# Vision tower on one core: the last group's depthwise taps read PSUM through a ring of eight banks, and token codes go row by row

## The chip, the cores and the metric

One core of a Trainium2 chip runs the kernel. The metric is device time in microseconds. The engines are called by their short names in rows: PE is TensorE (matmul), PEld its weight load, DVE is VectorE, ACT is ScalarE, POOL is GpSimd, SP is SyncE, whose work here is to issue transfers.

## The reference

Sixteen images of 3 x 256 x 256 are turned into 257 tokens of 256 features each: Sobel gradients in x and y, their hypotenuse, summed over the channels, and one class token ahead. Then comes one transformer layer: layer norm and attention for the 27 tokens of largest energy, then layer norm and a feed-forward net whose two products have quantized activations and ternary weights:

```python
h = bit_linear(x, w1)                                # 256 -> 1024 channels, codes in 8 bits
h = depthwise_conv1d(h.transpose(0, 2, 1), conv_w, conv_b)   # 3 taps along the tokens, one filter a channel
h = h.transpose(0, 2, 1)
h = jax.nn.silu(h)
return bit_linear(h, w2)                             # scale: 127 / max |h| over a token's 1024 channels
```

The second product can't begin before the maximum over all 1024 channels of a token is known, and the result is added to the residual.

## The kernel before

The images are worked on in 4 groups of 4 (`GB = 4`). The instruction streams of the engines are written out by hand, with semaphores between them. In the first three groups the attention and the feed-forward net of group g are interleaved with the gradients of group g + 1; the last group has nothing beside it. Its feed-forward net is a stage of its own, and its order is what the change touches.

Token codes: VectorE writes nine rows of int16 codes (`token_codes`, L1097 and L1098), one increment of `zi_ready` at the last. ScalarE scales the nine rows (`tokens_scaled`, L1522), one increment of `zs_ready`. TensorE transposes them, 16 transposes in four banks and two more for the class token's row (L1908 and L1911), and ScalarE evicts each bank into `zT` (L1528, L1533). This piece is the same in all four groups.

Hidden layer: there are 8 tiles of 128 channels for each image, 32 in the group. TensorE makes a tile of 128 channels by 257 tokens with 4 matmul instructions (L1727) in one of four banks (A0, A1, B0, B1). In groups 0 to 2 ScalarE evicts it and TensorE does the three taps as products with diagonal matrices. In the last group (`convolve=False`) the taps are done by the other engines. VectorE copies a tile into `gpad`, a padded buffer of four tiles (L946), and increments `gd_ready`. ScalarE reads the copy and makes the middle tap with scale and bias (L1410, `mid_ready`). VectorE adds the left and right taps out of `gpad` with `scalar_tensor_tensor` (the helper `stt`, L565). Tiles go in pairs: `TILE_SLOTS` lists two tiles for each of eight slots, and taps of a pair come one slot behind its copies. A loop of two rounds handles two images in each.

When the eight tiles of an image are done (`y_conv`), ScalarE applies SiLU to all of them in two instructions (L1374, and L1375 for the class token) and increments `f_ready`; `TAIL_SILU` sets the slots in which it does. VectorE reduces the image to maxima over its channels (`hidden_maxima`, L951). In a round the first image's maxima are taken at the round's end, and those of the second images wait until both rounds are over, in `ffn_quantize`:

```python
with dve.Fori(0, 2) as j:
    w = Chain(dve, vtiles, j * TILE_STEPS, lag=1)
    for k in range(len(TILE_SLOTS)):
        ffn_tiles(w, gl, j, k)
    hidden_maxima(gl, 2 * j)
    dve.wait_ge(y_conv, 2 * j + 2)
    settle()
ffn_quantize(step, gl, range(1, GB, 2), lambda: None, lambda: None)
```

`Chain` makes an engine wait for its own earlier instruction, with lag=1 for the one before the last. After the maxima TensorE transposes them (L1739), VectorE makes scales (L966 to L973), TensorE spreads these (L1746), VectorE makes codes, ScalarE converts them (L1254), TensorE does the second product (L1758), VectorE adds it to the residual and SyncE stores (L471).

Of the kernel before, what the change touches and what calls it, by code (L numbers as in the profile page):

```python
# [44 lines left out]
TILE_SLOTS = tuple((2 * k, 2 * k + 1) for k in range(8)) + ((),)  # L45
TAIL_SILU = (5, 8)
GB = 4
# [77 lines left out]
def tower_kernel(nc, x, cls_tok, w_in, b_qk, b_v, w_out, b_out, w1, conv_w, conv_b, w2, const, out):  # L125
# [4 lines left out]
    TILE_STEPS = 30  # L130
# [6 lines left out]
    with ExitStack() as ctx:  # L137
# [80 lines left out]
        s2B = fmax  # L218
        again()
# [116 lines left out]
        vnorm = sem("vnorm"); vtiles = sem("vtiles")  # L336
# [44 lines left out]
        y_conv = sem("y_conv"); f_ready = sem("f_ready")  # L381
# [162 lines left out]
        def _(dve):  # L544
# [375 lines left out]
            def ffn_tiles(w, gf, j, k):  # L920


                conv, scale = TILE_SLOTS[k - 1] if k > 0 else (), TILE_SLOTS[k]
                nt = (gf * GB + 2 * j) * FT
                for tap in (0, 2):
                    for i in conv:
                        t = i % FT
                        yd, gp = (ydw, ydw_odd)[i // FT][:, t, :], gpad[:, i % 4, tap:tap + S]
                        if tap == 0:
                            dve.wait_ge(mid_ready, 2 * j * FT + i + 1)  # L930
                            w(stt(yd, gp, cw[:, t, tap:tap + 1], yd, ALU.mult, ALU.add))
                            if len(conv) == 1:
                                w.all()
                        else:
                            if t == FT - 1:
                                w.all()
                            ins = stt(yd, gp, cw[:, t, tap:tap + 1], yd, ALU.mult, ALU.add)
                            if t == FT - 1:
                                ins.then_inc(y_conv, 1)
                            else:  # L940
                                w(ins)
                for i in scale:
                    if conv and i % 4 == conv[-1] % 4:
                        w.all()
                    dve.wait_ge(g_psum, nt + i + 1)
                    v.tensor_copy(gpad[:, i % 4, 1:S + 1], (A0, A1, B0, B1)[i % 4][:, 0:S]).then_inc(gd_ready, 1)  # L946

            def hidden_maxima(gf, b):

                dve.wait_ge(f_ready, gf * GB + b + 1)  # L950
                return v.tensor_reduce(fmax[:, :, bass.ds(b, 1), :].rearrange("p j o r -> p j (o r)"),  # L951
                                       f4[:, :, :, bass.ds(b, 1), :].rearrange("p t j o r -> p j (o r) t"), AX, ALU.max,
                                       apply_absolute_value=True)

            def ffn_quantize(step, gf, batches, meanwhile_1, meanwhile_2):

                am, sc, dq = small2[:, 0, :], small2[:, 1, :], small2[:, 2, :]
                for b in batches:
                    ins = hidden_maxima(gf, b)
# [118 lines left out]
            def token_codes(step, g):  # L1078
# [112 lines left out]
            for g in range(1, GROUPS):  # L1191
# [9 lines left out]
                ffn_quantize(step, gl, range(GB), lambda: norm_mean(norm_step, ROWS, g),  # L1201
# [37 lines left out]
        def _(act):  # L1239
# [164 lines left out]
            def ffn_tiles(gf, j, k):  # L1404

                nt = (gf * GB + 2 * j) * FT
                for i in TILE_SLOTS[k]:
# [4 lines left out]
                if k in TAIL_SILU:  # L1412
                    half = TAIL_SILU.index(k)
                    act.wait_ge(y_conv, 2 * j + half + 1)
                    silu(gf, 2 * j + half, half, (ydw, ydw_odd)[half])
# [216 lines left out]
            with act.Fori(0, 2) as j:  # L1632
                for k in range(len(TILE_SLOTS)):
                    ffn_tiles(gl, j, k)
# [5 lines left out]
        def _(pe):  # L1640
# [63 lines left out]
            def feed_forward(g, convolve):  # L1704
# [16 lines left out]
                for b in range(GB):  # L1721
                    for t in range(FT):
                        i = b * FT + t
                        if i >= 4:
                            pe.wait_ge(gd_ready, g * (GB * FT) + i - 3)
                        for k in range(DT):
                            ins = mm((A0, A1, B0, B1)[i % 4][:, 0:S], w1q[:, k, t * P:(t + 1) * P], zT[:, k, b, :],  # L1727
# [15 lines left out]
                pe.wait_ge(gd_ready, (g + 1) * (GB * FT))  # L1743
# [56 lines left out]
            def attention(g):  # L1800
# [103 lines left out]
                pe.wait_ge(zs_ready, g + 1)  # L1904
                for i in range(4):
                    t, k = i // 2, i % 2
                    for j in range(4):
                        ins = tr((T0, T1, B0, B1)[i][:, j * P:(j + 1) * P], zs[:, 4 * k + j, t * P:(t + 1) * P], ident)  # L1908
                    ins.then_inc(zT_psum, 1)
                for t in range(DT):  # L1910
# [55 lines left out]
```

## Time and profile before

| | |
|---|---|
| time, median of 3 runs | 1516.29 us (1515.9 to 1517.93) |
| the profiled execution's own time | 1519.31 us |
| its span | 1517.5 us |
| instructions | 11197 |
| busy, share of the span | VectorE 87%, TensorE 54%, ScalarE 48%, GpSimd 11% |
| chain that ended last | VectorE 45%, ScalarE 12%, transfers 10%, TensorE 10%, issue 7% |

A busy share is a mean over stages that differ: VectorE is at nine tenths or more in most slices of the first 1290 us, and far below that in the last group's attention and feed-forward net. The granted clock of TensorE is given as a share of 2.4 GHz: 1.00 is that, 0.50 is 1.2 GHz.

### The profile page before, as it was taken

To read this page: it belongs to the slowest core of one execution; us is meant where nothing else is said; L and a number is where in the kernel's file an instruction comes from. 1 tells how busy PE (TensorE), PEld (TensorE's weight loads), DVE (VectorE), ACT (ScalarE), POOL (GpSimd) and SP (SyncE) were. 2 spreads that over 40 slices of the span, in tenths; PEclk is the share of its full clock that TensorE was granted. 3 is DMA by queue.
4 is the path that set the end of the run, shared out by engine and by line. 5 is a ranking of instruction groups with operands and counts; after the bars stand their busy time and mean duration, and the time that the engine had idled before them with its cause. 6 is when DMAs were issued, how large, how long until landed. Compare 5 with 4: busy or idle time off the path is not lost.

```text
span 1517.5 us, 11197 instructions
## 1 busy us (share of the span) xinstructions
PE 815.9 (54%) x3334; PEld 645.1 (43%) x3334; DVE 1320.9 (87%) x2024; ACT 728.9 (48%) x1300; POOL 166.2 (11%) x208
## 2 busy tenths in 40 slices
PE   3564200457548743457647842556547842696644
PEld 1332100345437632446536732445436642585523
DVE  7999998898999999998999989998999999423576
ACT  2222333156386744156476744256476743332662
POOL 0000000013213000012313000012303000000000
PEclk8886655667669866567579866567679866877876
DMA  8000600017437510126528510126528010100001
GB/s 205 1 14 15 118 1 0 1 25 114 81 59 128 116 42 0 29 39 101 92 46 134 111 42 1 29 40 99 98 41 132 7 42 0 28 1 1 0 0 28
DMA packets 46380, 78.13 MB, mean 51 GB/s; under 512 B 7490, under 2 KB 31730, under 8 KB 44658
## 3 DMA queue, kind: packets, MB, share of 16 engines
q0 software_dynamic: 33408, 50.34, 20.4%
q1 hardware_dynamic: 12338, 26.31, 7.5%
q10 hardware_dynamic: 576, 0.79, 0.2%
q8 instruction: 26, 0.43, 0.1%
q14 instruction: 32, 0.26, 0.1%
HBM read 22.84 MB, written 4.25 MB: 18 GB/s over the span
## 4 chain that ended last, share of the span: by engine, by line
DVE 45%; ACT 12%; DMA 10%; PE 10%; issue 7%; POOL 0%; SPq 0%; DVEq 0%; ACTq 0%
DVE arena L562 16%; DVE arena L565 14%; DMA arena<-nrows_mem 3%; DMA arena<-img 3%; ACT arena L1374 2%; PE psum L1715 2%; PE psum L1809 2%; DMA arena<-h 2%; DMA arena<-zT 2%; ACT arena L1247 2%; DVE red L578 1%; ACT arena L1512 1%; DVE arena L951 1%; DVE arena L1049 1%; DVE out L565 1%
## 5 line engine op out<-in xcount | busy, mean ns | idle before, releaser
L562 DVE TENSOR_TENSOR arena<-arena 128x768 f32<-128x768 f32 (+2 forms) x519 | 477.4, 975 | 26.3 <-ACT arena L1289 22.5
L565 DVE SCALAR_TENSOR_TENSOR arena<-arena 128x768 f32<-128x768 f32 (+2 forms) x224 | 202.2, 956 | 0.1
L1727 PE MATMUL psum<-zT,w1q 128*128 128x257 f32 x512 | 142.2, 414 | 19.4 <-DVE gpad L946 14.8
L1727 PEld LDWEIGHTS psum<-zT,w1q 128*128 128x128 f32 x512 | 105.4, 208 | 42.9 <-DVE gpad L946 19.9
L1831 PE MATMUL psum<-arena 128*128 128x257 f32 x128 | 55.9, 612 | 71.6 <-ACT arena L1490 53.3
L538 POOL DMA_DIRECT2D h<-others x60 | 52.4, 873 | 375.2 <-DVE others L565 286.1
L1715 PE MATMUL psum<-gpad,win 128*128 128x257 f32 x288 | 77.1, 406 | 26.1 <-ACT gpad L1388 26.1
L1326 ACT ACTIVATE arena<-arena 128x768 f32<-128x768 int16 x32 | 27.0, 843 | 124.2 <-DVE arena L565 123.5
L565 DVE SCALAR_TENSOR_TENSOR arena<-img 128x768 f32<-128x768 f32 x74 | 67.7, 954 | 9.0 <-DMA img<-x 8.7
L1715 PE MATMUL psum<-gpad,onehotT 128*128 128x257 f32 x216 | 58.0, 413 | 31.0 <-ACT gpad L1388 31.0
L1247 ACT ACTIVATE arena<-arena 128x256 f32<-128x256 f32 x65 | 23.3, 409 | 106.6 <-DVE arena L565 68.3
L1715 PEld LDWEIGHTS psum<-gpad,win 128*128 128x128 f32 x288 | 57.3, 202 | 38.7 <-ACT gpad L1388 29.8
L1831 PEld LDWEIGHTS psum<-arena 128*128 128x128 f32 x128 | 37.8, 310 | 84.4 <-ACT arena L1490 57.4
L951 DVE TENSOR_REDUCE arena<-arena 128x288 f32<-128x2304 f32 (+1 forms) x16 | 64.9, 4098 | 8.7 <-ACT arena L1375 8.5
L499 POOL DMA_DIRECT2D arena<-nrows_mem x18 | 15.6, 865 | 514.6 <-ACT arena L1298 442.2
L1391 ACT ACTIVATE xT<-psum,cb 128x257 f32<-128x257 f32 x96 | 45.5, 474 | 40.7 <-PE psum L1715 40.7
L1480 ACT ACTIVATE arena<-psum,arena 128x257 f32<-128x257 f32 x64 | 29.5, 473 | 68.0 <-DVE arena L1050 68.0
L1715 PEld LDWEIGHTS psum<-gpad,onehotT 128*128 128x128 f32 x216 | 44.3, 208 | 40.8 <-ACT gpad L1388 33.7
L565 DVE SCALAR_TENSOR_TENSOR arena<-arena,others 128x768 f32<-128x768 int16 x64 | 58.3, 953 | 0.0
L1662 PE MATMUL psum<-img,cst 128*128 128x512 f32 (+1 forms) x28 | 16.0, 713 | 73.2 <-DVE arena L565 73.2
L1374 ACT ACTIVATE arena<-xT 128x2048 f32<-128x2048 f32 (+1 forms) x14 | 55.2, 3941 | 0.2
L1775 PE MATMUL psum<-cst,arena 128*128 128x128 f32 x64 | 15.3, 402 | 73.7 <-DVE e L562 71.7
(235 smaller groups left out, 2121.6 us busy)
## 6 DMA issues: line engine op xcount, KB each, us to landing
arena<-nrows_mem POOLq DMA_DIRECT2D x36, 384.0 KB, 7.2
arena<-img POOLq DMA_DIRECT2D x36, 384.0 KB, 7.6
img<-x SPq DMA_DIRECT2D x36, 258.0 KB, 7.5
h<-others POOLq DMA_DIRECT2D x60, 128.0 KB, 2.7
arena<-arena POOLq DMA_DIRECT2D x18, 384.0 KB, 8.8
arena<-zT POOLq DMA_DIRECT2D x12, 384.0 KB, 8.4
out<-out SPq DMA_DIRECT2D x16, 256.0 KB
img<-x SPq DMA_DIRECT2D x48, 64.5 KB, 7.0
```

The source lines that it names most:

```text
L538: pool.dma_start(h9[:, row, :], others[:, row % 2, c, :], accum_op=ALU.add).then_inc(row_sums, 16)
L562: return v.tensor_tensor(o, a, b, op)
L565: return v.scalar_tensor_tensor(out=o, in0=a, scalar=s, in1=b, op0=op0, op1=op1)
L951: return v.tensor_reduce(fmax[:, :, bass.ds(b, 1), :].rearrange("p j o r -> p j (o r)"), f4[:, :, :, bass.ds(b, 1), :].rearrange("p t j o ...
L1247: ins = s.activation(ln[1][:, j, :], src(j), ACT.Square)
L1374: s.activation(fb[:, :, 0:ROWS, :], yd[:, :, 1:S].rearrange("p t (r j) -> p t j r", j=ROWS), ACT.Silu)
L1391: s.activation(ydw[:, t, :], (C0, C1, T0, T1)[i % 4][:, 0:S], ACT.Identity, bias=cb[:, t:t + 1]).then_inc(conv_taken, 1)
L1480: s.activation(attn[:, hg, :], (C0, C1, T0, T1)[hg][:, 0:S], ACT.Exp, scale=0.25, bias=sm[:, 1, hg:hg + 1], accum_out=sm[:, 2, hg:hg + 1]) ...
L1715: ins = mm((C0, C1, T0, T1)[i % 4][:, 0:S], diagonal(t, k), gpad[:, i % 4, k:k + S], start=(k == 0), stop=(k == 2))
L1727: ins = mm((A0, A1, B0, B1)[i % 4][:, 0:S], w1q[:, k, t * P:(t + 1) * P], zT[:, k, b, :], start=(k == 0), stop=(k == DT - 1))
L1809: ins = mm(C0[:, t * P:(t + 1) * P], y_row(j)[:, t * P:(t + 1) * P], rhs, start=(j == 0), stop=(j == ROWS))
L1831: mm((C0, C1, T0, T1)[hg][:, 0:S], qbd[:, hg // 2, 4 * (hg % 2):4 * (hg % 2) + 4, :].rearrange("p h q -> p (h q)"), kT[:, b % 2, hg // 2, ...
```

## The change

There are four edits. (1) In the last group TensorE puts its tiles in all eight banks in turn (`RING = 8`) and waits for `tile_done` of the tile eight before. The copy into `gpad` is gone: ScalarE's middle tap and VectorE's outer taps read the bank; the outer taps cover 256 columns. (2) The loop of two rounds is written out. SiLU of an image comes after the middle tap of tile 5 of the next image (`SILU_LAG = 5`), and its maxima after tile 7 of the next image. (3) The last image's SiLU and its maxima are made in two halves of four tiles each, and the two maxima are joined by one more instruction. (4) In all groups each row of token codes and each scaled row has its own increment and wait, and the transposes take rows 0 to 3 of both halves of the features first, then rows 4 to 7.

```diff
-TILE_SLOTS = tuple((2 * k, 2 * k + 1) for k in range(8)) + ((),)
-TAIL_SILU = (5, 8)
+RING = 8
+SILU_LAG = 5
...
+            def last_tiles(w, gf):
+                for i in range(0, GB * FT, 2):
+                    for j in (i, i + 1):
+                        t, g, y = j % FT, banks[j % RING], (ydw, ydw_odd)[j // FT % 2][:, j % FT, :]
+                        dve.wait_ge(mid_ready, j + 1)
+                        w(stt(y[:, 1:S], g[:, 0:S - 1], cw[:, t, 0:1], y[:, 1:S], ALU.mult, ALU.add))
+                    for j in (i, i + 1):
+                        t, g, y = j % FT, banks[j % RING], (ydw, ydw_odd)[j // FT % 2][:, j % FT, :]
+                        if j == i + 1:
+                            w.all()
+                        stt(y[:, 0:S - 1], g[:, 1:S], cw[:, t, 2:3], y[:, 0:S - 1], ALU.mult, ALU.add).then_inc(tile_done, 1)
+                    if i > FT and i % FT == FT - 2:
+                        w(hidden_maxima(gf, i // FT - 1))
...
+            def last_maxima(gf):
+                b, half = GB - 1, FT // 2
+                whole = fmax[:, :, b:b + 1, :]
+                dve.wait_ge(f_ready, gf * GB + GB)
+                image_maxima(fmax_low, b, slice(0, half)).then_inc(half_max, 1)
+                dve.wait_ge(f_ready, gf * GB + GB + 1)
+                image_maxima(whole, b, slice(half, FT)).then_inc(half_max, 1)
+                dve.wait_ge(half_max, 2)
+                return tt(whole, whole, fmax_low, ALU.max)
...
                 for row in range(ROW9):
-                    ins = v.tensor_scalar(zi[:, row, :], out9[:, row, :], nmean[:, row:row + 1], sc[:, row:row + 1],
-                                          ALU.add, ALU.mult)
-                ins.then_inc(zi_ready, 1)
+                    v.tensor_scalar(zi[:, row, :], out9[:, row, :], nmean[:, row:row + 1], sc[:, row:row + 1],
+                                    ALU.add, ALU.mult).then_inc(zi_ready, 1)
...
-            with dve.Fori(0, 2) as j:
-                w = Chain(dve, vtiles, j * TILE_STEPS, lag=1)
-                for k in range(len(TILE_SLOTS)):
-                    ffn_tiles(w, gl, j, k)
-                hidden_maxima(gl, 2 * j)
-                dve.wait_ge(y_conv, 2 * j + 2)
-                settle()
-            ffn_quantize(step, gl, range(1, GB, 2), lambda: None, lambda: None)
+            w = Chain(dve, vtiles, lag=1)
+            last_tiles(w, gl)
+            w.all()
+            ffn_quantize(step, gl, [lambda: last_maxima(gl)], lambda: None, lambda: None)
...
+            def last_tiles(gf):
+                nt = gf * (GB * FT)
+                for i in range(GB * FT):
                     t = i % FT
-                    act.wait_ge(gd_ready, nt + i + 1)
-                    s.activation((ydw, ydw_odd)[i // FT][:, t, :], gpad[:, i % 4, 1:S + 1], ACT.Identity,
+                    act.wait_ge(g_psum, nt + i + 1)
+                    s.activation((ydw, ydw_odd)[i // FT % 2][:, t, :], banks[i % RING][:, 0:S], ACT.Identity,
                                  scale=cw[:, t, 1:2], bias=cb[:, t:t + 1]).then_inc(mid_ready, 1)
+                    if i >= FT and i % FT == SILU_LAG:
+                        b = i // FT - 1
+                        act.wait_ge(tile_done, (b + 1) * FT)
+                        silu(gf, b, b % 2, (ydw, ydw_odd)[b % 2])
+                for half in range(2):
+                    act.wait_ge(tile_done, GB * FT - FT // 2 * (1 - half))
+                    silu_half(gf, GB - 1, half)
...
-                act.wait_ge(zi_ready, g + 1)
                 for row in range(ROW9):
-                    ins = s.activation(zs[:, row, :], zi[:, row, :], ACT.Copy, scale=token[:, 7, row:row + 1])
-                ins.then_inc(zs_ready, 1)
+                    act.wait_ge(zi_ready, g * ROW9 + row + 1)
+                    s.activation(zs[:, row, :], zi[:, row, :], ACT.Copy, scale=token[:, 7, row:row + 1]).then_inc(zs_ready, 1)
...
-                        if i >= 4:
+                        if convolve and i >= 4:
                             pe.wait_ge(gd_ready, g * (GB * FT) + i - 3)
+                        if not convolve and i >= RING:
+                            pe.wait_ge(tile_done, i - RING + 1)
+                        bank = (A0, A1, B0, B1)[i % 4] if convolve else banks[i % RING]
...
-                pe.wait_ge(zs_ready, g + 1)
                 for i in range(4):
-                    t, k = i // 2, i % 2
+                    k, t = i // 2, i % 2
+                    pe.wait_ge(zs_ready, g * ROW9 + 4 * k + 4)
```

## Rows read from the trace of the kernel before

**Rows 1.** Timeline, codes to the first hidden tile: start us, us, engine, line

```profile
1401.18 3.00 DVE L1098 TENSOR_SCALAR onehot<-out,token 128x256 int16<-128x256 f32 x9
...
1404.21 3.70 ACT L1522 ACTIVATE arena<-onehot,token 128x256 f32<-128x256 int16 x9 [4.51 <-DVE onehot L1098]
...
1407.97 3.68 PE L1908 MATMUL psum<-cst,arena 128*128 128x128 f32 x16 [15.46 <-ACT arena L1522]
1409.12 3.87 ACT L1528 ACTIVATE zT<-psum 128x512 f32<-128x512 f32 x4 [1.21 <-PE psum L1908]
...
1412.79 0.22 ACT L1533 ACTIVATE zT<-psum 128x4 f32<-128x4 f32 x2
...
1413.15 7.17 PE L1727 MATMUL psum<-zT,w1q 128*128 128x257 f32 x32 [1.09 <-ACT zT L1533]
```

**Rows 2.** Timeline, end of the hidden layer of the last group

```profile
1473.21 8.13 DVE L951 TENSOR_REDUCE arena<-arena  x2
...
1481.26 4.01 DVE L951 TENSOR_REDUCE arena<-arena 128x288 f32<-128x2304 f32 x1
1485.32 1.78 PEld L1739 LDWEIGHTS psum<-cst,arena 128*128 128x128 f32 x9 [22.42 <-DVE arena L951]
```

**Rows 3.** Windows: PE, PEld, DVE, ACT, POOL busy us (instructions), clock, DMA share

```profile
1413.00:1446.00 33.00, 21.25 (x81) 15.99 (x82) 24.59 (x52) 20.17 (x26) 0.00 (x0) 0.90 0.00 0
...
1120.00:1245.00 125.00, 83.23 (x347) 69.78 (x347) 118.77 (x142) 81.72 (x137) 19.50 (x24) 0.81 0.31 55
```

**Rows 4.** Timeline, one period of a pair of tiles

```profile
1420.23 0.75 DVE L946 COPY gpad<-psum 128x257 f32<-128x257 f32 x2
1420.69 1.09 ACT L1410 ACTIVATE xT<-gpad,cb,cw 128x257 f32<-128x257 f32 x2 [1.69 <-DVE gpad L946]
...
1421.33 1.77 DVE L565 SCALAR_TENSOR_TENSOR xT<-gpad,cw,xT 128x257 f32<-128x257 f32 x4 [0.34 <-ACT xT L1410]
1423.02 0.75 DVE L946 COPY gpad<-psum 128x257 f32<-128x257 f32 x2
```

**Rows 5.** VectorE's waits from 1413 to 1486: us in total, times, longest

```profile
DVE arena L565 <- ACT arena L1410: 10.5, 8, 4.3
DVE xT L565 <- ACT xT L1410: 4.2, 8, 1.9
```

**Rows 6.** Waits from 1120 to 1245, in the third group

```profile
ACT arena L1342 <- DVE arena L562: 5.6, 2, 3.5
...
DVE arena L951 <- ACT arena L1375: 2.4, 1, 2.4
```

**Rows 7.** Page, costliest groups: busy us, mean ns, idle before

```profile
L1391 ACT ACTIVATE xT<-psum,cb 128x257 f32<-128x257 f32 x96 | 45.5, 474 | 40.7 <-PE psum L1715 40.7
```

**Rows 8.** Line L565 by operands: ns min/median/max, first and last start

```profile
L565 DVE SCALAR_TENSOR_TENSOR arena<-arena,small x131: 475/480/485, 247.8 to 1282.8; 128x256 f32<-128x256 f32 x131
...
L565 DVE SCALAR_TENSOR_TENSOR out<-psum,small,out x36: 474/476/484, 610.1 to 1510.3; 128x256 f32<-128x256 f32 x36
```

**Rows 9.** Timeline, the result added to the residual out of PSUM

```profile
1507.13 3.62 DVE L565 SCALAR_TENSOR_TENSOR out<-psum,small,out 128x256 f32<-128x256 f32 x9 [1.68 <-PE psum L1758]
```

**Rows 10.** Timeline around the first SiLU of the last group

```profile
1430.31 1.28 ACT L1374 ACT_TABLE_LOAD   x1
...
1431.61 3.88 ACT L1374 ACTIVATE arena<-xT 128x2048 f32 x1
...
1435.93 1.08 ACT L1410 ACTIVATE arena<-gpad,cb,cw 128x257 f32<-128x257 f32 x2
...
1438.71 3.79 PE L1727 MATMUL psum<-zT,w1q 128*128 128x257 f32 x8 [4.71 <-DVE gpad L946]
```

**Rows 11.** Timeline, a strided reduction in the third group

```profile
1238.06 3.61 DVE L572 TENSOR_REDUCE red<-h 128x128 f32<-128x2048 f32 x1
```

**Rows 12.** Windows around the first hidden matmuls, columns as in rows 3

```profile
1408.00:1412.00 4.00, 4.00 (x18) 3.67 (x18) 0.00 (x0) 2.88 (x4) 0.00 (x0) 0.50 0.00 0
1412.70:1434.00 21.30, 17.17 (x72) 13.20 (x72) 15.52 (x38) 11.93 (x18) 0.00 (x0) 1.00 0.00 0
```

More of the change, by code:

```diff
@@ L129, in tower_kernel @@
     G_STEPS = 46
-    TILE_STEPS = 30
     IMG_IN = 16 * 2 * GB * CH
@@ L218, in tower_kernel @@
         s2B = fmax
+        fmax_low = take(ROW9 * SLOTS).rearrange("p (j o r) -> p j o r", j=ROW9, o=1)
         again()
@@ L334, in tower_kernel @@
         gpad_zero = sem("gpad_zero")
-        vnorm = sem("vnorm"); vtiles = sem("vtiles")
+        vnorm = sem("vnorm"); vtiles = sem("vtiles"); tile_done = sem("tile_done")
+        half_max = sem("half_max")
         h_saved = sem("h_saved")
@@ L380, in tower_kernel @@
         gd_ready = sem("gd_ready"); mid_ready = sem("mid_ready")
-        y_conv = sem("y_conv"); f_ready = sem("f_ready")
+        f_ready = sem("f_ready")
         fmax_ready = sem("fmax_ready"); fmaxT_psum = sem("fmaxT_psum"); fmaxT_taken = sem("fmaxT_taken")
@@ L918, in first_group @@
                 u.all()
[L920 to L946, printed above, removed]
@@ L948, in hidden_maxima, with image_maxima @@
+            def image_maxima(room, b, tiles):
+                return v.tensor_reduce(room.rearrange("p j o r -> p j (o r)"),
+                                       f4[:, tiles, :, b:b + 1, :].rearrange("p t j o r -> p j (o r) t"), AX, ALU.max,
+                                       apply_absolute_value=True)
             def hidden_maxima(gf, b):
                 dve.wait_ge(f_ready, gf * GB + b + 1)
-                return v.tensor_reduce(fmax[:, :, bass.ds(b, 1), :].rearrange("p j o r -> p j (o r)"),
-                                       f4[:, :, :, bass.ds(b, 1), :].rearrange("p t j o r -> p j (o r) t"), AX, ALU.max,
-                                       apply_absolute_value=True)
@@ L955, in ffn_quantize @@
-            def ffn_quantize(step, gf, batches, meanwhile_1, meanwhile_2):
+                return image_maxima(fmax[:, :, b:b + 1, :], b, slice(0, FT))
+            def last_maxima(gf):
[7 more added lines that the diff above has]
+                return tt(whole, whole, fmax_low, ALU.max)
@@ L957, in ffn_quantize @@
+            def ffn_quantize(step, gf, image_peaks, meanwhile_1, meanwhile_2):
                 am, sc, dq = small2[:, 0, :], small2[:, 1, :], small2[:, 2, :]
-                for b in batches:
-                    ins = hidden_maxima(gf, b)
+                for peak in image_peaks:
+                    ins = peak()
                 ins.then_inc(fmax_ready, 1)
@@ L1199, in _ @@
                 magnitude_rows(g, 3, lambda k: None)
-                ffn_quantize(step, gl, range(GB), lambda: norm_mean(norm_step, ROWS, g),
+                ffn_quantize(step, gl, [lambda b=b: hidden_maxima(gl, b) for b in range(GB)], lambda: norm_mean(norm_step, ROWS, g),
                              lambda: norm_variance(norm_step, ROWS, g * 2 + 1))
@@ L1402, in tap_diagonals, with silu_half @@
                 ins.then_inc(diagonals, 1)
-            def ffn_tiles(gf, j, k):
-                nt = (gf * GB + 2 * j) * FT
-                for i in TILE_SLOTS[k]:
+            def silu_half(gf, b, half):
+                tiles = slice(half * FT // 2, (half + 1) * FT // 2)
+                fb, yd = f4[:, tiles, :, b:b + 1, :].rearrange("p t j o r -> p t j (o r)"), ydw_odd[:, tiles]
+                s.activation(fb[:, :, 0:ROWS, :], yd[:, :, 1:S].rearrange("p t (r j) -> p t j r", j=ROWS), ACT.Silu)
+                s.activation(fb[:, :, ROWS, :], yd[:, :, 0:1].to_broadcast([P, FT // 2, BLK]), ACT.Silu).then_inc(f_ready, 1)
+            def last_tiles(gf):
+                nt = gf * (GB * FT)
+                for i in range(GB * FT):
                     t = i % FT
-                    act.wait_ge(gd_ready, nt + i + 1)
-                    s.activation((ydw, ydw_odd)[i // FT][:, t, :], gpad[:, i % 4, 1:S + 1], ACT.Identity,
+                    act.wait_ge(g_psum, nt + i + 1)
+                    s.activation((ydw, ydw_odd)[i // FT % 2][:, t, :], banks[i % RING][:, 0:S], ACT.Identity,
                                  scale=cw[:, t, 1:2], bias=cb[:, t:t + 1]).then_inc(mid_ready, 1)
[L1412 to L1415, printed above, removed]
+                    if i >= FT and i % FT == SILU_LAG:
[5 more added lines that the diff above has]
+                    silu_half(gf, GB - 1, half)
             def ffn_scales(gf):
@@ L1631, in _ @@
             tokens_scaled(gl)
-            with act.Fori(0, 2) as j:
-                for k in range(len(TILE_SLOTS)):
-                    ffn_tiles(gl, j, k)
+            last_tiles(gl)
             ffn_scales(gl)
@@ L1742, in feed_forward @@
                 pe.wait_ge(diag2_ready, g + 1)
-                pe.wait_ge(gd_ready, (g + 1) * (GB * FT))
+                if convolve:
+                    pe.wait_ge(gd_ready, (g + 1) * (GB * FT))
+                else:
+                    pe.wait_ge(tile_done, GB * FT)
                 for k in range(3):
@@ L1902, in attention @@
                     ins.then_inc(res_psum, 1)
-                pe.wait_ge(zs_ready, g + 1)
                 for i in range(4):
-                    t, k = i // 2, i % 2
+                    k, t = i // 2, i % 2
+                    pe.wait_ge(zs_ready, g * ROW9 + 4 * k + 4)
                     for j in range(4):
@@ L1909, in attention @@
                     ins.then_inc(zT_psum, 1)
+                pe.wait_ge(zs_ready, g * ROW9 + ROW9)
                 for t in range(DT):
```

2 lines of the change are left out of this document (1 added, 1 removed).

## The prediction

> **What bounds the kernel now.** I read the chain that ended last first: in the final 105 us the kernel has no next group to overlap with, so each stage there is on the path, while in the three groups before VectorE is nearly always busy. Then I took stage windows, the table of waits, and the timeline of the last group's hidden layer, which runs from the first matmul at 1413.15 to the last maximum at 1485.27: 72.1 us [rows 1, 2]. There no engine is full: in the first half VectorE works 24.6 of 33 us, TensorE 21.3, ScalarE 20.2 [rows 3]. What is seen instead is a handover. A pair of tiles takes 2.79 us (copy at 1420.23, next at 1423.02): 0.75 of copies, then 0.34 waiting for ScalarE's middle tap, then 1.68 of four outer taps [rows 4]. ScalarE reads the copy, so VectorE must copy first. Beside that each SiLU stops the taps, since ScalarE makes no middle taps meanwhile; the sum of VectorE's waits for it is 14.7 us, longest 4.3 [rows 5], and two reductions stand in a row at the end [rows 2]. In front of the stage lies a strictly serial piece: 9 code rows on VectorE, then 9 on ScalarE, then 18 transposes, then four evictions, 1401.18 to 1413.0 [rows 1].
>
> **Token codes row by row.** The first code row is done at 1401.6 instead of the ninth at 1404.2. ScalarE needs 3.70 for nine rows (0.40 apart), more than VectorE's 3.00, so it ends at 1401.63 + 3.70 = 1405.33, not 1407.91 [rows 1]. The order of transposes is changed to row halves: the first eight need rows 0 to 3, done at 1403.3; eight at 0.23 each end at 1405.2, the next eight at 1407.1, the two of row 8 at 1407.5. ScalarE evicts in order behind its ninth row: two quarters at once from 1405.3, 0.92 apart as now (four of 1.12 in 3.87), the third at 1407.2 at the latest, the fourth at 1408.1, then the two small ones: end about 1409.35. TensorE starts the hidden matmuls at 1409.45, **3.7 us** earlier than 1413.15. The added increments sit on instructions that are there anyway, and the added waits are met in order: behind ScalarE's wait for a row stand only the later rows and evictions. I cost them at nothing. In groups 0 to 2 the same 3.7 us are gained by ScalarE and TensorE but not by VectorE: ScalarE falls back into step at its next squares and roots, where it waits 5.6 us in all for VectorE's line L562 alone [rows 6]. So zero there. Bounds: VectorE's only wait at the group's end is 2.4 us (2.5 and 3.7 in the other two groups, of the same view), but the work that sets it starts after that 5.6 us wait, so I don't count it.
>
> **The ring and the dropped copies.** Removed: 32 copies (0.42 each, 0.32 to 0.43 on the engine [rows 4]), their handover, the loop with its settle memsets, and table loads at the loop's head. Added: nothing per tile; ScalarE's middle tap reads PSUM (0.47 for a like eviction with bias only [rows 7], 0.60 as now from SBUF; I take 0.50), VectorE's taps read PSUM and cover 256 columns. The trace has that form: 0.476 from PSUM against 0.480 from SBUF [rows 8], so the pitch of 0.42 (1.68 for four [rows 4]) stays; bounds are 0.39 (nine of the PSUM form in the last 3.62 us of VectorE's work: its pitch [rows 9]) and 0.48, no overlap at all. With clock full, TensorE needs 7.17/32 x 4, less its first fill, = 0.87 per tile [rows 1]. Now the recurrence, t = 0 at the first matmul. P is a tile's end in PSUM, M its middle tap, D its outer taps.
>
> Tiles 0 to 13: P13 = 1.1 + 13 x 0.87 = 12.4, M13 = 12.9. Taps of a pair cost 1.68 against TensorE's 1.74, so VectorE keeps up, one pair behind. Then SiLU of image 0: table load 1.28, and 4.32 from its start to the next middle tap (1431.61 to 1435.93 [rows 10]); M14 = 12.9 + 1.3 + 4.3 + 0.5 = 19.0. VectorE idles from 14.2 to 19.0: the one large stall that stays. TensorE fills the ring to tile 21 meanwhile.
>
> From 19.0 VectorE is the bound. Pair 7 ends at 20.7, maxima of image 0 take 4.06 [rows 2] to 24.8; ScalarE uses these to run to tile 21 (21.8), and does SiLU 1 until 26.1 with the table still loaded, hidden behind pairs 8 to 10, which end at 29.8. Pair 11 finds its middle taps (27.1) and ends at 31.5; maxima 1 to 35.6. The ring refills as pairs 8 to 11 free banks (26 to 31.5); even at half clock, 1.71 per tile (8 instructions in 3.79 [rows 10]), tile 29 is there by 36.8. At full clock M29 is at 34 and SiLU 2 ends at 38.3, before pair 15 starts at 40.6. Pairs 12 to 15 end at 42.3, maxima 2 at 46.4. The half SiLUs of image 3 (about 2.3 each, half of 4.32 and a fixed part) run from 39.2 and from 42.4, ended by 44.8: hidden. Last: two half reductions and one maximum of 288 elements. A strided reduction of 2048 elements to 128 costs 3.61 [rows 11], one of 2304 to 288 costs 4.02 [rows 2]: the price goes with elements, so 2.1 each; if it went with outputs, up to 2.8 each. 46.4 + 4.2 + 0.5 = **51.1**.
>
> **The clock.** When the transposes began at 1407.97 the granted clock was 0.50, and 1.00 from 1412.7 [rows 12], so the first hidden matmul ran at 2.4 GHz. Now they begin at about 1403.4 with a 2 us hole before the hidden matmuls. The clock may be up already, or rise up to 4.7 us into them. Each us at 1.2 GHz delays M13 by half a us: 0 to 2.3, I take **0.9**. A half clock later in the stage is covered by VectorE up to SiLU 2, see (d).
>
> The stage thus ends at 1409.45 + 51.1 + 0.9 = 1461.45 against 1485.27: **23.8 us** less, of which 3.7 from the token codes, about 20 from the ring. What follows (transposes of the maxima, scales, second product, store) is unchanged, after an idle TensorE in both. The sum against the profiled execution: 1519.3 - 23.8 = 1495.5 (span 1517.5, 1.8 around it). That execution was 3.0 above the median of the runs, so **1492.5** for the median.
>
> **A rule against the change.** Rows show PSUM no dearer than SBUF as a source of a VectorE tap, 0.476 against 0.480 [rows 8]. The Trainium skill ("VectorE: DVE Perf Modes", section "Rules for kernel authors") advises to copy PSUM to SBUF first where many operations follow, and its table in the section on the TRN2 errata gives a PSUM source 62 cycles more than an SBUF one, 65 ns as an estimate; over the 36 taps from pair 7 on that would be 2.3 us, a time of 1494.8. The rows disagree with the price, and by them the advice fails here: two taps and a middle tap don't repay a copy.
>
> **Rivals.** (a) Ring starved: the clock stays at 1.2 GHz. Then P29 = 2.1 + 29 x 1.71 = 51.7, SiLU 2 ends at 56.5, pair 15 at 58.7, and 4.1 + 4.2 + 0.5 more is 67.5, 16.4 over: 1508. Against it: 1.00 through 21 us with TensorE busy 17.2 of them [rows 12]. For it: 0.50 after each SiLU's hole [rows 10, 12]. (b) Table loads stay around each SiLU: +1.3 before M14, hidden at SiLU 1 (29.2 against 29.8), some 1.2 at SiLU 2: 1495. Against it: ScalarE goes from SiLU to the middle tap at 1435.93 without a load [rows 10]. (c) The other side: taps from PSUM get slow while ScalarE evicts and TensorE writes neighbouring banks. All 64 would have to cost 0.37 more, 0.80 in place of 0.42, to eat 24 us; beyond that it is slower, at 1.0 each it is 64 x 0.58 - 23.8 = 13 slower, 1529. Against it, copies from PSUM at 0.43 with TensorE writing [rows 4]; for it only that no tap has done this beside ScalarE. That the written-out loop starves for instructions has no sign in the earlier groups, which are written out too: VectorE is 118.8 of 125 us busy there [rows 3]. (d) The cover fails: SiLU 2 is late by TensorE at half clock (M29 37.4, M31 42.7): +1.5 to 2, in the range.
>
> **Numbers.** Forecast with (d) 0.80; (b) 0.07; (a) or part of it, 1498 to 1508, 0.08; (c) 0.03; gains beyond the sum (earlier groups' 2.4 to 3.7, faster pitch) 0.02. Low end: pitch 0.39 (-1.1), no clock loss (-0.9), middle taps and half reductions a bit cheaper (-0.5), rounded down to 1489. High end: clock +1.4, pitch 0.48 (+2.2), reductions by outputs (+1.4), together 1497.5, rounded to 1498. 0.2% is 3 us, about what a measurement here can tell from no change. Faster 0.96, same 0.02, slower 0.02.
>
> **What would show it.** Hidden matmuls start 3.7 us earlier after the codes. VectorE shows no copies, one wait of 4.5 to 5 us for the first SiLU, then is over 95% busy until the last maxima. Taps 0.48 long, 0.42 apart. One table load in the stage. The stage takes about 52 us; the last reductions are two of 2.1. It would be wrong if taps on PSUM are longer, if VectorE waits again at the second or third SiLU, or if the clock row reads 0.50 through the first 14 tiles.

## The result and the profile after

The changed kernel takes 1491.49 us (median of 4 runs, 1488.19 to 1494.95) against 1517.11 (1515.9 to 1518.31): a ratio of 0.9831, 95% interval 0.98 to 0.9862, 25.6 us less. (The before side is the three runs of the section on the time before and a fourth, 1518.31, which moves its median from 1516.29.) The changed kernel's runs lie in two pairs, 1488.2 and 1488.5, 1494.4 and 1494.95, so its median is a value between them that no run had. The profiled execution took 1488.19, of the lower pair; its span is 1486.4, 31.1 less than before.

The windows of the last group, columns as in [rows 3]: attention from the first energy maximum to the first code row, codes to the first hidden matmul, hidden layer to the transposes of the maxima, and the rest.

```profile
1291.82:1395.64 103.82, 80.86 (x371) 67.48 (x371) 30.41 (x79) 35.09 (x102) 0.00 (x0) 0.80 0.05 11
1395.64:1403.69 8.05, 4.10 (x19) 3.71 (x19) 3.00 (x10) 7.45 (x15) 0.00 (x0) 0.60 0.00 0
1403.69:1454.19 50.50, 29.88 (x128) 25.01 (x129) 42.79 (x70) 35.50 (x46) 0.00 (x0) 0.86 0.00 0
1454.19:1486.40 32.21, 16.25 (x99) 13.41 (x99) 17.70 (x27) 10.67 (x11) 0.00 (x0) 0.71 0.14 33
```

Of the 31.1 us, the hidden layer gives 21.7 (72.2 before, 1413.15 to 1485.33 in [rows 1, 2]) and the codes 3.9 (11.97 before [rows 1]). These two make 25.6. That the medians differ by the same 25.6 is partly chance, since one of them lies between two pairs. The other 5.5 of this execution lie ahead of the codes of the last group: 1.4 before its attention begins, and 4.2 in that attention (107.98 before), where nothing was changed; the experiments and the part on the sum come back to this.

The timeline of the codes, where ScalarE now starts 0.44 after VectorE and TensorE before ScalarE is through:

```profile
1395.64 3.00 DVE L1103 TENSOR_SCALAR onehot<-out,token 128x256 int16<-128x256 f32 x9
1396.08 3.70 ACT L1532 ACTIVATE arena<-onehot,token 128x256 f32<-128x256 int16 x9 [1.93 <-DVE onehot L1103]
1397.84 3.67 PE L1921 MATMUL psum<-cst,arena 128*128 128x128 f32 x16 [10.89 <-ACT arena L1532]
...
1399.69 3.83 ACT L1537 ACTIVATE zT<-psum 128x512 f32<-128x512 f32 x4
```

And of the hidden layer:

```profile
1403.69 19.30 PE L1737 MATMUL psum<-zT,w1q 128*128 128x257 f32 x88 [1.74 <-ACT zT L1542]
...
1416.68 1.28 ACT L1374 ACT_TABLE_LOAD   x1
1417.98 3.90 ACT L1374 ACTIVATE arena<-xT 128x2048 f32<-128x2048 f32 x1
...
1422.90 1.79 DVE L566 SCALAR_TENSOR_TENSOR arena<-psum,cw,arena 128x256 f32<-128x256 f32 x4 [4.87 <-ACT arena L1417]
...
1428.71 6.36 DVE L566 SCALAR_TENSOR_TENSOR xT<-psum,cw,xT 128x256 f32<-128x256 f32 x16
...
1439.08 6.36 DVE L566 SCALAR_TENSOR_TENSOR arena<-psum,cw,arena 128x256 f32<-128x256 f32 x16
...
1445.34 8.30 DVE L940 TENSOR_REDUCE arena<-arena 128x288 f32<-128x2304 f32 x3
1445.47 2.07 ACT L1408 ACTIVATE arena<-arena 128x1024 f32<-128x1024 f32 x1 [0.60 <-DVE arena L566]
1447.44 0.29 ACT L1409 ACTIVATE arena<-arena 128x128 f32<-128x128 f32 x1
1453.68 0.46 DVE L563 TENSOR_TENSOR arena<-arena 128x288 f32<-128x288 f32 x1
```

TensorE makes 22 tiles (88 instructions) in one go, the ring's eight beyond tile 13. After the first tile VectorE has one long wait, 4.87 us for the first SiLU. From 1422.9 it works without a gap: 16 taps in 6.36 are 0.39 apart, the three reductions at 1445.34 are one of 4.1 and two of 2.1. The taps by operands, ns min/median/max: from SBUF in the first row, from PSUM in the second. They are as long as each other, as in [rows 8]:

```profile
L566 DVE SCALAR_TENSOR_TENSOR arena<-arena,small x131: 476/480/485, 247.8 to 1281.4; 128x256 f32<-128x256 f32 x131
...
L566 DVE SCALAR_TENSOR_TENSOR arena<-psum,cw,arena x32: 474/482/484, 1412.7 to 1445.0; 128x256 f32<-128x256 f32 x32
```

### The profile page after: what moved, and what is told of

Same layout as the page of the kernel before. It is cut to its first block and busy times, and to the rows that moved or that the text cites. A ratio compares the mean times of both kernels' runs of the same rounds, so it can differ in the third digit from the quotient of the medians.

```text
span 1486.4 us, 10993 instructions
## 1 busy us (share of the span) xinstructions
PE 815.6 (55%) x3334; PEld 647.2 (44%) x3334; DVE 1308.0 (88%) x1992; ACT 722.3 (49%) x1298; POOL 166.3 (11%) x208
## 3 DMA queue, kind: packets, MB, share of 16 engines
HBM read 22.84 MB, written 4.25 MB: 18 GB/s over the span
## 5 line engine op out<-in xcount | busy, mean ns | idle before, releaser
L563 DVE TENSOR_TENSOR arena<-arena 128x768 f32<-128x768 f32 (+3 forms) x520 | 477.4, 969 | 26.1 <-ACT arena L1289 22.3
L1737 PE MATMUL psum<-zT,w1q 128*128 128x257 f32 x512 | 137.2, 406 | 12.3 <-ACT zT L1542 7.2
L1722 PE MATMUL psum<-gpad,win 128*128 128x257 f32 x288 | 82.7, 429 | 33.6 <-ACT gpad L1388 33.6
L1722 PEld LDWEIGHTS psum<-gpad,win 128*128 128x128 f32 x288 | 60.5, 214 | 47.8 <-ACT gpad L1388 37.3
L1788 PE MATMUL psum<-cst,arena 128*128 128x128 f32 x64 | 15.3, 401 | 73.7 <-DVE e L563 71.7
L1374 ACT ACTIVATE arena<-xT 128x2048 f32<-128x2048 f32 x14 | 55.3, 3951 | 0.2
```

Of the source, the lines that this page charges most:

```text
L563: return v.tensor_tensor(o, a, b, op)
L1374: s.activation(fb[:, :, 0:ROWS, :], yd[:, :, 1:S].rearrange("p t (r j) -> p t j r", j=ROWS), ACT.Silu)
L1722: ins = mm((C0, C1, T0, T1)[i % 4][:, 0:S], diagonal(t, k), gpad[:, i % 4, k:k + S], start=(k == 0), stop=(k == 2))
L1737: ins = mm(bank[:, 0:S], w1q[:, k, t * P:(t + 1) * P], zT[:, k, b, :], start=(k == 0), stop=(k == DT - 1))
```

## The experiments

Lengths in each profiled execution, from windows with the same four borders, and times. The ratio is to the kernel before on the same chip.

| kernel | attention | codes | hidden layer | rest | time, median (range, runs) | ratio, 95% interval |
|---|---|---|---|---|---|---|
| changed | 103.8 | 8.05 | 50.5 | 32.2 | 1491.49 (1488.19 to 1494.95, 4) | 0.9831 (0.98 to 0.9862) |
| e1 codes only | 108.0 | 8.04 | 73.8 | 33.0 | 1517.31 (1510.7 to 1517.9, 10) | 0.9997 (0.9985 to 1.001) |
| e2 ring only | 108.0 | 11.98 | 50.5 | 32.1 | 1495.46 (1492.29 to 1497.75, 4) | 0.9853 (0.9832 to 0.9874) |
| e3 ring of 4 | 103.8 | 8.05 | 62.5 | 32.8 | 1502.74 (1502.11 to 1503.51, 4) | 0.991 (0.9893 to 0.9926) |
| e4 last image whole | 108.0 | 8.07 | 52.1 | 32.1 | 1488.95 (1488.4 to 1494.74, 4) | 0.9816 (0.9799 to 0.9832) |
| e5 copies kept | 103.8 | 8.07 | 71.3 | 32.2 | 1514.82 (1509.21 to 1515.89, 10) | 0.9975 (0.9962 to 0.9988) |
| e6 table first | 108.0 | 8.05 | 50.7 | 32.6 | 1488.26 (1487.42 to 1494.1, 4) | 0.9803 (0.9788 to 0.9818) |
| e7 first SiLU split | 103.8 | 8.07 | 47.4 | 32.2 | 1486.11 (1485.2 to 1487.34, 4) | 0.9792 (0.9777 to 0.9808) |
| e8 all three | 103.8 | 8.06 | 46.6 | 32.2 | 1485.11 (1484.58 to 1485.82, 5) | 0.9786 (0.9772 to 0.9799) |
| e9 busy, before | 107.9 | 11.98 | 72.1 | 32.2 | 1518.64 (1509.53 to 1522.11, 10) | 0.9989 (0.997 to 1.0008) |
| e10 busy, codes only | 107.9 | 8.04 | 73.7 | 33.0 | 1516.15 (1506.49 to 1519.75, 10) | 0.9971 (0.9951 to 0.999) |
| e11 busy, changed | 105.5 | 8.04 | 52.5 | 32.2 | 1491.93 (1486.19 to 1494.58, 4) | 0.9814 (0.9788 to 0.984) |
| e12 busy, all three | 107.9 | 8.04 | 48.2 | 32.2 | 1486.58 (1479.58 to 1492.86, 6) | 0.9781 (0.9753 to 0.9809) |

**e1, the codes alone.** The kernel before with the increments and waits by row, as in the diff's parts for edit (4); two places of it:

```diff
-                ins.then_inc(zi_ready, 1)
+                                    ALU.add, ALU.mult).then_inc(zi_ready, 1)
...
-                act.wait_ge(zi_ready, g + 1)
+                    act.wait_ge(zi_ready, g * ROW9 + row + 1)
```

> The kernel before with only the token codes taken row by row; the hidden layer keeps its copies, four banks and its loop. Theory: the piece from the first code row to the first hidden matmul shrinks from 11.97 us to 8.05, as in the changed kernel's trace, so 3.9 us less, and groups 0 to 2 give nothing: about 1513.2. Rival: the earlier groups gain too (their last maxima wait 2.4 to 3.7 us for SiLU), which would show as 6 us or more in all. Second rival, for the spread of the changed kernel's times: the granted clock in the last group's attention, which this edit doesn't touch, moves the total by some 4 us either way, so totals scatter over 5 to 7 us while the piece is 8.05 in every trace.

The piece is 8.04 as expected, but the time falls by 0.5 us, and the interval includes none. The trace shows where the 3.9 us went. Windows of codes, hidden layer and rest:

```profile
1400.98:1409.02 8.04, 4.10 (x18) 3.71 (x19) 3.00 (x10) 7.57 (x16) 0.00 (x0) 0.50 0.00 0
1409.02:1482.80 73.78, 36.02 (x129) 26.54 (x129) 55.55 (x102) 40.04 (x48) 0.00 (x0) 0.80 0.00 0
1482.80:1515.80 33.00, 17.15 (x99) 13.96 (x99) 17.71 (x27) 10.67 (x11) 0.00 (x0) 0.66 0.13 32
...
1409.00:1412.00 3.00, 2.98 (x7) 2.44 (x8) 0.43 (x1) 1.60 (x2) 0.00 (x0) 0.50 0.00 0
```

The hidden layer begins at 1.2 GHz, where it began at 2.4 before [rows 12]: its first eight tiles take 8.78 us for 7.17, and the stage is 1.6 longer; the rest is 0.8 longer at a clock of 0.66 for 0.71. So 2.4 of 3.9 are given back in this execution. By the median 3.4 were; what the other runs did, no trace shows.

The gap of TensorE before the hidden matmuls doesn't decide this. The changed kernel has the same transposes at 1.2 GHz and the same gap of 1.74 us, and began at 2.4 GHz:

```profile
1403.60:1422.30 18.70, 18.61 (x86) 16.37 (x87) 11.72 (x28) 13.48 (x18) 0.00 (x0) 1.00 0.00 0
```

What goes with it is the attention ahead. Of the eight traces with row by row codes and no added products, the five whose attention took 103.8 us (changed, e3, e5, e7, e8) begin the hidden layer at 2.4 GHz, and the three in which it took 108.0 (e1, e4, e6) begin it at 1.2. The two kinds thus differ by more than the attention. The profiled executions of e1, e4 and e6, all of 108.0, took 1517.61, 1494.74 and 1494.1, and the lowest times of the same kernels are 6.3 to 6.9 us shorter, like the two pairs of the changed kernel; that those are executions of the other kind fits, but no trace shows it.

**e2, the ring alone.** The changed kernel with those parts of the diff undone.

> The changed kernel with the token codes as before, nine rows and then nine rows. Theory: the hidden layer from its first matmul to the last maximum takes 50.4 us as in the changed kernel and not 72.1, so 21.7 less than before: about 1495.4; the edits add up (3.9 + 21.7 = 25.6 measured together). Rival: they overlap, the earlier start of the hidden layer being worth less without the other; then this one alone gives over 23 or under 20.

22.3 us less by the medians, stage 50.5. The part of edits (1) to (3) is confirmed and doesn't depend on the codes.

**e3, a ring of four.**

```diff
-RING = 8
+RING = 4
```

> The changed kernel with RING = 4, so TensorE waits for the outer taps of the tile four before. Theory by the recurrence in tiles (0.87 for a tile, 0.46 for a middle tap, 0.395 for an outer one, 4.32 for a SiLU, 4.06 for maxima): the first 14 tiles are unchanged; TensorE stands still during the maxima of images 0 and 1, ScalarE can't run ahead before SiLU 1 and 2, and VectorE waits some 3.7 us at each: 58.6 in place of 50.4, about 8 us slower than the changed kernel, near 1500. Rival: the depth buys nothing because VectorE is full anyway and four tiles are 1.6 us of its work: within 1 us of the changed kernel. Dropping the copies alone then gives the whole gain.

The depth is needed, and worth more than I had worked out: 12.0 us in the stage, 11.3 by the medians. VectorE waits 16.3 us after the first tiles where the changed kernel waits 4.87, which is 11.4 of the 12.0. Its waits (in total, times, longest) and two rows of the timeline:

```profile
DVE arena L566 <- ACT arena L1417: 10.6, 6, 4.8
DVE xT L566 <- ACT xT L1417: 5.7, 4, 3.5
```

```profile
1426.11 3.80 PE L1737 MATMUL psum<-zT,w1q 128*128 128x257 f32 x8 [4.64 <-DVE arena L566]
...
1431.66 8.38 PE L1737 MATMUL psum<-zT,w1q 128*128 128x257 f32 x24 [1.76 <-DVE xT L566]
```

My 8 us had TensorE at 2.4 GHz. It stands still 4.64 us, and its next 8 instructions take 3.80 where 2.00 is usual. With four banks nothing covers that.

**e4, the last image whole.**

```diff
-                for half in range(2):
-                    act.wait_ge(tile_done, GB * FT - FT // 2 * (1 - half))
-                    silu_half(gf, GB - 1, half)
+                act.wait_ge(tile_done, GB * FT)
+                silu(gf, GB - 1, 1, ydw_odd)
...
-            ffn_quantize(step, gl, [lambda: last_maxima(gl)], lambda: None, lambda: None)
+            ffn_quantize(step, gl, [lambda: hidden_maxima(gl, GB - 1)], lambda: None, lambda: None)
```

> The changed kernel with the last image's SiLU and maxima in one piece, no join. Theory: the halves hide nothing, since in the changed kernel VectorE is still at the maxima of image 2 (to 1449.4) when the second half SiLU ends (1447.7); a whole SiLU from 1445.5 would end at 1449.8 and one reduction of 4.02 follows: 1453.9 against 1454.14, so 0.2 to 0.4 us less by the trace and no measurable difference in time. Rival: the split is worth the 2 us of half a SiLU that it takes off the end, and this kernel is 2 us slower in the stage.

The end of the stage:

```profile
1452.21 4.18 DVE L940 TENSOR_REDUCE arena<-arena 128x288 f32<-128x2304 f32 x1
1452.33 3.94 ACT L1374 ACTIVATE arena<-arena 128x2048 f32<-128x2048 f32 x1 [1.40 <-DVE arena L566]
...
1456.70 4.02 DVE L940 TENSOR_REDUCE arena<-arena 128x288 f32<-128x2304 f32 x1 [0.31 <-ACT arena L1375]
```

VectorE waits 0.31 us for the whole SiLU: it lies under the maxima of image 2. From the start of those to the transposes are 8.57 us, and in the changed kernel 8.85 (1445.34 to 1454.19). So in these traces the halves cost 0.3 and hide nothing. The stage of this trace is longer because its first matmuls ran at 1.2 GHz: the first middle tap comes 2.09 after the first matmul (1.14 in the changed kernel), the table load of the first SiLU 14.58 (12.99), 1.6 lost. With that off it is 50.5, as in the changed kernel, so the stage as a whole doesn't show the 0.3. The three lower times are at 1488.4 to 1489.0. The time alone can't tell it from the changed kernel.

**e5, the copies kept.** Ring, order and written-out loop as changed; the copy to `gpad` is back and the taps read it.

```diff
+                        dve.wait_ge(g_psum, gf * GB * FT + j + 1)
+                        v.tensor_copy(gpad[:, j % 4, 1:S + 1], banks[j % RING][:, 0:S]).then_inc(gd_ready, 1)
...
-                        w(stt(y[:, 1:S], g[:, 0:S - 1], cw[:, t, 0:1], y[:, 1:S], ALU.mult, ALU.add))
+                        w(stt(y, g, cw[:, t, 0:1], y, ALU.mult, ALU.add))
```

> The changed kernel's ring of eight banks, its written-out loop and its places for SiLU and maxima, but VectorE copies each tile to the four padded buffers as before, and all three taps read the copy. Theory: a pair of tiles is back at 2.79 us (0.75 copies, 0.34 handover, 1.68 taps), ScalarE is never more than one pair ahead, so each of three SiLUs stops VectorE: 16 x 2.79 + about 5.5 + 2 x 2.3 + 12.2 + 4.7 = about 71, near the 72.1 of before; the gain is the copies and what they block. Rival: the order (maxima one image later, ring) brings half of the 21.7 us by itself: about 61.

71.3, as expected. Ring, order and loop without the dropped copy give 0.9 of 21.7 us. VectorE again waits at each of the first three SiLUs: 4.22, 2.85 and 2.80 us (before: 4.27, 1.91 and 4.25). Two of them:

```profile
1430.19 1.83 DVE L566 SCALAR_TENSOR_TENSOR arena<-gpad,cw,arena 128x257 f32<-128x257 f32 x4 [4.22 <-ACT arena L1428]
...
1447.44 1.83 DVE L566 SCALAR_TENSOR_TENSOR xT<-gpad,cw,xT 128x257 f32<-128x257 f32 x4 [2.85 <-ACT xT L1428]
```

With the copy in this place the ring does almost nothing, since ScalarE can only start from what VectorE has copied. Of the 20.8 us between this kernel and the changed one 12.0 are the copies' own time (16 pairs of 0.75), and 8.6 are waits (13.5 us against 4.9).

One rival was not run. Before and here, the copies of a pair stand behind the taps of the pair ahead, so the next thing VectorE needs is a middle tap that ScalarE has only begun: this is the 0.34 in each pair. Copies put in front of those taps, or a `gpad` deeper than four tiles, might win back a part of the 8.6 us with the copies kept. So e5 shows that the order and the ring alone give next to nothing (0.9 us); that the copy must go for any gain isn't shown. e3 shows that without the copy the depth decides over half of the gain.

**e6, the table first.**

```diff
                 nt = gf * (GB * FT)
+                s.activation(idle[:, 0:1], cb[:, 0:1], ACT.Silu)
```

> The changed kernel with one SiLU of a single column put before the first middle tap, while ScalarE waits 1.3 us for the first hidden tile. Theory: the table load (1.28) goes there, the first SiLU starts at once, and VectorE's stall before tile 14 falls from 4.87 to 3.6: stage 49.1 in place of 50.4, 1.3 us less. Rival: ScalarE's stall is not what VectorE waits for but the tiles behind it; then the stall stays 4.9. If the load lies on the first middle tap it costs up to 0.1.

The stall is 3.5 (changed kernel: 4.87):

```profile
DVE arena L566 <- ACT arena L1418: 3.5, 1, 3.5
```

The stage reads 50.7, since here too the first two tiles came at 1.2 GHz: the first middle tap is 2.09 after the first matmul. Its first SiLU starts 14.48 after the first matmul where 13.0 would follow from the changed kernel's, so 1.5 is the clock's and 49.2 is left, an estimate that agrees with the forecast of 49.1. The time can't tell: the three lower runs are at 1487.42 to 1488.6, beside 1488.2 and 1488.5.

**e7, the first SiLU in halves** (last image whole).

```diff
-                    if i >= FT and i % FT == SILU_LAG:
+                    if i in (SILU_LAG, FT + SILU_LAG):
+                        half = i // FT
+                        act.wait_ge(tile_done, FT // 2 * (half + 1))
+                        silu_half(gf, 0, half, ydw)
+                    elif i >= FT and i % FT == SILU_LAG:
```

> The changed kernel with the first image's SiLU in two halves, after middle taps 5 and 13, and the last image's whole. Theory: the first half (table load 1.3 and 2.4) stops VectorE for 3 us at tile 6, in which TensorE fills the ring, so that ScalarE is then ahead of VectorE and the second half is hidden: one stall of 3.0 in place of one of 4.9, stage about 47.5 to 48 in place of 50.4. Rival: the stalls add up (3.0 + 2.3) and the stage is 50.5 or more.

47.4, 3.1 less than the changed kernel (up to 0.3 of it from the last image), and 1486.11 by the time. One stall buys ScalarE its lead, and the second half is free.

**e8, all three.**

> Table load first, first SiLU in halves, last image whole. Theory: VectorE's stalls are 1.7 and 0.5: stage 46.8, 3.6 us less than the changed kernel, about 1488 where that is 1491.5, but by the time alone hard to tell, since the clock in the attention before it scatters the total by 6 us; the trace's stage tells it. Rival: VectorE is then waiting for TensorE at its clock or for the ring, and the stage stays above 49.

46.6, with waits of 1.27 and 0.45 for the two halves. It is the best of all at 1485.11 (ratio to before 0.9786), 6.4 us under the changed kernel's median; part of that is the kind of execution, attention 103.8 here and in e7, while the changed kernel's runs seem to be of both kinds. Against its lower pair, 1488.2 and 1488.5, it is 3.1 to 3.4 us, and the stage is 3.9 shorter.

**e9 to e12, TensorE kept busy in two holes.** Products of constants that nothing reads are added in the last group's attention: to the kernel before (e9), to e1's (e10), to the changed one (e11) and to e8's (e12).

```diff
+                if g == GROUPS - 1:
+                    for _ in range(14):
+                        mm(T0[:, 0:D], ident, cst[:, 0:D], start=True, stop=True)
                 pe.wait_ge(onehot_ready, g + 1)
...
+                if g == GROUPS - 1:
+                    for _ in range(22):
+                        mm(A1[:, 0:D], ident, cst[:, 0:D], start=True, stop=True)
```

> The kernel before, with products of constants into banks that are free, in two holes of TensorE in the last group: 14 while it waits for the one-hot rows, 22 while it waits for the scaled code rows. Nothing reads their results. Theory: the last group's attention takes either 103.8 or 108.0 us by the state of the clock at its first products; with TensorE busy up to them it is 103.8 or less in every run, and the times of all runs lie within 1.5 us: about 1513 to 1514. Rival: the clock falls all the same in the 1 to 3 us between the last added product and the wanted ones, and both values still occur, or the added products run over the hole at 1.2 GHz and delay the attention by up to 8 us.

> The same added products in the kernel with row by row codes alone. In its plain form the codes gave 0.5 us of time although 3.9 in the trace, because the hidden layer then began at 1.2 GHz (stage 73.8 against 72.2) and the end had a lower clock too. Theory: with TensorE busy before the transposes the stage starts at 2.4 GHz and the 3.9 us come through: 3.5 to 4 less than the kernel before with added products. Rival: the loss has nothing to do with the clock ahead of the stage; the difference of the two stays under 1.5 us.

> The same added products in the changed kernel. Theory: hidden layer 50.5 in every run and attention 103.8, so the two values of the time (1488.4 and 1494.7) become one near 1487 to 1488.5. Against the kernel before with added products it is 25.6 us less. Rival: times still fall in two groups 6 us apart.

> The same added products in the kernel with the table load first, the first SiLU in halves and the last image whole, which took 1485.1 with the attention at 103.8 in its trace. Theory: nothing left to repair but the transposes of the codes, now at 2.4 GHz but behind ScalarE's evictions: 1483 to 1485. Rival: the added products collide with the waits and cost 1 us or more.

My theory of a cure fell in all four. Times scatter more, 12.6 us in e9 against 7.5 of the kernel before on the same chip. In e12 they scatter by 13.3 against 1.2 in e8, but that was on another chip, and the kernel before scatters by 4.6 there. The medians don't move beyond their spread. e11 shows what happened in the last hole. TensorE's timeline and windows of codes and hidden layer:

```profile
1400.53 1.09 PE L1927 MATMUL psum<-cst,arena 128*128 128x128 f32 x8 [1.38 <-ACT arena L1532]
1402.12 1.09 PE L1927 MATMUL psum<-cst,arena 128*128 128x128 f32 x8 [0.50 <-ACT arena L1532]
1403.05 0.38 PE L1931 MATMUL psum<-cst,arena 128*128 128x128 f32 x2
1406.36 6.00 PE L1737 MATMUL psum<-zT,w1q 128*128 128x257 f32 x19 [2.93 <-ACT zT L1542]
```

```profile
1398.32:1406.36 8.04, 3.23 (x23) 2.35 (x21) 3.00 (x10) 7.44 (x15) 0.00 (x0) 1.00 0.00 0
1406.36:1458.82 52.46, 33.13 (x129) 27.33 (x129) 42.94 (x70) 35.42 (x46) 0.00 (x0) 0.79 0.00 0
```

The clock was 1.00 through the transposes, which then were over sooner; ScalarE's evictions set the pace, so TensorE idled 2.93 us instead of 1.74 and the hidden layer began at 1.2 GHz all the same, as in e10 and e12 behind gaps of 2.92 and 2.93. In the attention the first products now ran at 2.4 GHz, and it took 107.9, 107.9, 105.5 and 107.9. Why, is open. e10 against e9 is 2.5 us less by the medians, in between the two theories and within the scatter; the stage of 73.7 has the loss that the added products were to cure.

## Why the prediction was right

**The codes.** 3.7 forecast, 3.92 measured: ScalarE's last eviction needed no wait for the transposes. That nothing would come in groups 0 to 2 holds. The last group begins at 1291.82 and not 1293.2, but this goes with the kind of execution and not with the edit. VectorE's code rows in the second and third group, before and then changed:

```profile
780.45 3.00 DVE L1098 TENSOR_SCALAR onehot<-out,token 128x256 int16<-128x256 f32 x9
1120.57 3.00 DVE L1098 TENSOR_SCALAR onehot<-out,token 128x256 int16<-128x256 f32 x9
```

```profile
780.36 3.00 DVE L1103 TENSOR_SCALAR onehot<-out,token 128x256 int16<-128x256 f32 x9
1117.96 3.00 DVE L1103 TENSOR_SCALAR onehot<-out,token 128x256 int16<-128x256 f32 x9
```

That stretch is 340.1 before and 337.6 changed. It is 337.6 to 337.8 in the five traces with attention 103.8 and 340.1 in the five with 108.0, e1, e4 and e6 with the edited codes among them; the stretch from there to the last group is 1.2 longer in the five short ones (173.9 against 172.6). From the codes of group 0 to the last group, traces of 108.0 take 851.5 us without the edit and 851.3 to 851.4 with it: 0.1 to 0.3 at most is the edit's.

**The hidden layer.** 51.1 by the recurrence, 50.5 measured. The terms: stall at the first SiLU 4.8, measured 4.87; pairs of taps 1.68, measured 1.57 to 1.58, near the lower bound of the pitch (36 taps x 0.03, some 1 us less; the sum was 0.6 over); half reductions 2.1 each, measured 2.1, so the price goes with elements; later SiLUs hidden, as they were. The middle tap from PSUM takes 0.56, nearer its upper neighbour. The prediction gave the step from four banks to eight no price of its own; e3 puts it at 12.0. The step that e5 confirms is the main one: with the copies back, a pair takes 2.83 again. One reading was loose: the 14.7 us of waits [rows 5] are not the SiLUs' alone. Those cause 10.4 (4.27, 1.91, 4.25), and twelve handovers of 0.34 are the rest.

**The clock.** I took 0.9 between 0 and 2.3. With the codes row by row it is 0 in the five traces with attention 103.8 and 1.5 to 1.6 in the three with 108.0; no trace has 0.9, which was a middle of two values. What I missed is that executions come in two kinds that differ by some 6 us: 4.2 in the attention, the 1.5 here, and about 0.6 before the last group (1.3 in the changed kernel's trace).

**The rivals.** (a) was not seen with eight banks; e3 has it in part, after TensorE's stops. (b) no: one table load. (c) no: taps 0.482 from PSUM with both neighbours at work. The rule of the Trainium skill ("VectorE: DVE Perf Modes", "Rules for kernel authors"), to copy first when many operations follow, would have cost 20.8 us here with the copy in e5's place. The 65 ns more for a PSUM source, the prediction's estimate from the same page's table on the TRN2 errata, isn't there: 0.482 beside 0.480. (d) did not occur: SiLU 2 ended at 1441.6, before VectorE came to pair 15.

**The sum.** 1492.5 was forecast, 1491.49 came; 23.8 less by the two stages against 25.6. That the two times lie within 1 us is partly luck. The lower pair, 1488.2 and 1488.5, lies below my range, and the upper one inside it; the median of four falls between. The forecast was worked out from an execution with attention 108.0, and for one like it the sum before the step to the median said 1495.5; the upper pair, which fits that kind, came to 1494.4 and 1494.95. What is right without luck is the stages. The profiled execution's 31.1 holds 5.5 that I don't put down to the change. The attention of the last group takes 103.8 us in five and 108.0 in five of the ten traces in which its code is that of before, at a mean clock of 0.80 against 0.78 or 0.75. In e2's trace:

```profile
1293.32:1401.32 108.00, 80.88 (x371) 67.71 (x371) 30.41 (x79) 35.13 (x102) 0.00 (x0) 0.78 0.04 10
```

What puts an execution on the one or the other is open; the traces part before 1120 us. No trace of the kernel before is of the 103.8 kind, so what the change gives between two executions of that kind isn't shown. Open too is why e7 and e8 kept within 2.1 us. The codes alone gained little in nine of ten runs, 1516.5 to 1517.9, and the profiled one shows how the gain is lost; the tenth, 1510.7, may be of the other kind and doesn't show that the codes gained there.

## What to carry to other kernels

When two engines need the same tile, ask whether the second waits for a copy by the first: the copy costs its own time and the second engine's lead. Here, with it gone, the ring began to work. Its depth must cover the longest block on the consumer (4 us of maxima, some five tiles at 0.87): eight banks did, four didn't and brought TensorE's stops back with a slow clock; depths between were not run. Splitting work pays where an engine waits for it (the first SiLU, 3.1 us) and costs where other work lies over it (the last, 0.3). And a gain of 4 us ahead of matmuls must be read in the stage behind it, as the clock can take half of it back (2.4 of 3.9 in e1). Where times come in two levels, compare traces of the same level before taking a median's difference for the change's.

## What the runs showed of the hardware

A gap of 2.93 us of TensorE, with a granted clock of 1.00 ahead of it, was followed by 0.55 early in the hidden layer (e11, 1407 to 1410); in the changed kernel a gap of 1.74 after transposes at 1.2 GHz was followed by 1.00, and in e1, e4 and e6 the same gap (1.74 to 1.76) after the same transposes was followed by 0.50. So the length of the gap alone doesn't tell the clock behind it. Work added to keep TensorE busy in the holes didn't keep the clock up where it mattered. Neither VectorE nor ScalarE was slowed by reading PSUM while TensorE wrote other banks: 0.482 a tap beside 0.480 from SBUF, and 0.56 a middle tap against 0.60 from SBUF.
